# Second FFN of a macaron layer: the next pair's layer norm right behind the first pair's layers, the second tile's down products between the up layers, two table loads moved

## What is computed

```python
x = x + 0.5 * _L0_ffn_ref(_layernorm(x), ...)
x = x + _L0_attn_ref(_layernorm(x), ...)
x = x + 0.5 * _L0_ffn_ref(_layernorm(x), ...)

# the FFN: D_IN 128, D_HID 512
h = jax.nn.silu(_tlin(x, w1_w, w1_s)) * _tlin(x, w2_w, w2_s)
h = jax.nn.gelu(_tlin(h, h1_w, h1_s), approximate=False)
h = jax.nn.gelu(_tlin(h, h2_w, h2_s), approximate=False)
return _tlin(h, w3_w, w3_s)
```

## Time and profile before

| | before |
|---|---|
| median of three runs | 442.1 us |
| the profiled execution, as a run | 442.02 us |
| its span in the trace | 440.3 us |
| PE matmul busy | 371.1 us, 84% |
| DVE busy | 294.8 us, 67% |
| ACT busy | 277.7 us, 63% |
| POOL busy | 41.9 us, 10% |
| chain that ended last | PE 58%, DVE 26%, issue 7%, ACT 7%, DMA 1% |

### The profile page before, as it was taken

One profiled execution on the slowest core, in us unless ns is written; L12 is line 12 of the kernel. 1 busy time (PEld: TensorE's weight loads), 2 busy tenths in 40 slices (PEclk: granted clock), 3 DMA queues, 4 the chain that ended last, 5 costly groups with the idle time before them and its releaser, 6 DMA issues.

```text
span 440.3 us, 9783 instructions
## 1 busy us (share of the span) xinstructions
PE 371.1 (84%) x4132; PEld 278.6 (63%) x4132; DVE 294.8 (67%) x461; ACT 277.7 (63%) x434; POOL 41.9 (10%) x103
## 2 busy tenths in 40 slices
PE   5599999999999998899488489366599687978996
PEld 3377776678866876799377376233267465556885
DVE  2796679628216845699696968667868696578433
ACT  4788956879677776383243265451576838558973
POOL 4000000000000100000788400000000000000000
PEclk9899999999999996889956889585999898989999
DMA  8900007400000000071600001600000000001001
GB/s 272 333 1 2 2 0 227 111 1 1 1 1 0 0 2 3 4 214 49 173 5 4 1 4 36 230 1 1 0 1 3 1 0 2 0 1 49 3 1 48
DMA packets 14325, 19.75 MB, mean 45 GB/s; under 512 B 960, under 2 KB 9152, under 8 KB 14272
## 3 DMA queue, kind: packets, MB, share of 16 engines
q1 hardware_dynamic: 14128, 18.94, 14.4%
q10 hardware_dynamic: 144, 0.01, 0.0%
HBM read 17.91 MB, written 1.05 MB: 43 GB/s over the span
## 4 chain that ended last, share of the span: by engine, by line
PE 58%; DVE 26%; issue 7%; ACT 7%; DMA 1%; DVEq 0%; SPq 0%; ACTq 0%
PE ps_a L723 11%; PE ps_a L724 11%; PE ps_a L827 8%; PE ps_a L894 2%; PE ps_a L884 2%; DVE arena L1074 2%; DVE arena L1071 2%; PE ps_d L794 2%; PE ps_d L858 2%; PE ps_a L917 2%; DVE acts L1121 2%; PE ps_d L724 2%; PE ps_d L723 2%; PE ps_d L894 2%; DVE hbuf L1116 2%
## 5 line engine op out<-in xcount | busy, mean ns | idle before, releaser
L723 PE MATMUL ps_a<-acts,w_f 128*128 128x512 f32 x256 | 103.6, 405 | 9.1 <-ACT acts L597 8.5
L724 PE MATMUL ps_a<-acts,w_f 128*128 128x512 f32 x256 | 101.7, 397 | 0.0
L723 PEld LDWEIGHTS ps_a<-acts,w_f 128*128 128x128 f32 x256 | 49.2, 192 | 22.6 <-ACT acts L597 10.2
L724 PEld LDWEIGHTS ps_a<-acts,w_f 128*128 128x128 f32 x256 | 49.2, 192 | 10.9 <-issue 0.7
L597 ACT ACTIVATE acts<-ps_a,vec 128x512 fp32r<-128x512 f32 x64 | 44.6, 697 | 0.0
L827 PE MATMUL ps_a<-xnp,conv_w 128*128 128x512 f32 x156 | 38.5, 404 | 0.0
L1140 DVE TENSOR_TENSOR acts<-gbuf,acts 128x512 fp32r<-128x512 f32 x32 | 21.6, 689 | 24.9 <-ACT acts L597 24.9
L1140 DVE TENSOR_TENSOR acts<-ghbuf,acts 128x512 fp32r<-128x512 f32 x32 | 21.2, 689 | 20.8 <-ACT acts L597 20.8
L827 PEld LDWEIGHTS ps_a<-xnp,conv_w 128*128 128x128 f32 x156 | 29.3, 188 | 8.2 <-issue 1.4
L987 DVE SCALAR_TENSOR_TENSOR arena<-ps_d,arena 128x512 f32<-128x512 f32 x16 | 11.0, 686 | 30.4 <-ACT arena L551 26.3
L594 ACT ACTIVATE gbuf<-ps_a,vec 128x512 f32<-128x512 f32 x32 | 22.3, 697 | 10.3 <-PE ps_a L724 10.2
(11 more groups left out here) (211 smaller groups left out, 778.5 us busy)
## 6 DMA issues: line engine op xcount, KB each, us to landing
toep<-in_fir SPq DMA_DIRECT2D x24, 288.0 KB, 6.5
w_in<-in_h SPq DMA_DIRECT2D x4, 1024.0 KB, 8.2
g_rows<-in_gW SPq DMA_DIRECT2D x4, 640.0 KB, 6.7
w_in<-in_w SPq DMA_DIRECT2D x6, 256.0 KB, 4.7
iobuf<-in_x SPq DMA_DIRECT2D x4, 256.0 KB, 6.5
toep<-in_taps SPq DMA_DIRECT2D x1, 768.0 KB, 6.7
y<-iobuf SPq DMA_DIRECT2D x3, 256.0 KB, 2.4
toep<-in_proj SPq DMA_DIRECT2D x1, 256.0 KB, 8.6
```

Source lines behind the costliest of these rows:

```text
L723: e.matmul(bank, w, hi, start=start, stop=False)
L724: return e.matmul(bank, w, lo, start=False, stop=stop)
```

## The change

The list of steps of the second FFN is rewritten at the turn from the first pair to the second, and two preloads are put into ACT's walk. Afterwards the steps are: mean 2, var 2, mean 3, var 3, down 0, up 2, down 1, out 0, out 1, up 3, and then as before. ACT loads the table of the reciprocal root ahead of `mean` of tile 2 and the table of silu behind `var` of tile 3. A side effect in unchanged code: where `mean` and `var` of a tile stand next to each other, DVE's L988 frees both their banks at once.

```diff
         else:
-            s += [("up", f, a)] + ([("out", f, 0), ("out", f, 1)] if last else []) + [("up", f, b)]
+            s += [("up", f, a)] + ([("down", f, 1), ("out", f, 0), ("out", f, 1)] if last else []) + [("up", f, b)]
         if more and last:
 
-            s += [("hid1", f, a), ("hid1", f, b), ("hid2", f, a), ("wo", 2, 2), ("wo", 2, 3), ("hid2", f, b), ("down", f, a),
-                  ("mean", f, 2), ("mean", f, 3), ("var", f, 2), ("var", f, 3), ("down", f, b)]
+            s += [("hid1", f, a), ("hid1", f, b), ("hid2", f, a), ("wo", 2, 2), ("wo", 2, 3), ("hid2", f, b),
+                  ("mean", f, 2), ("var", f, 2), ("mean", f, 3), ("var", f, 3), ("down", f, a)]
@@
                 elif kind == "mean":
                     n = NORM_AT[s]
+                    if s == ("mean", 1, 2):
+                        preload(ACT.Abs_reciprocal_sqrt)
@@
+                    if s == ("var", 1, 3):
+                        preload(ACT.Silu)
```

## The result

The changed kernel took 445.69 us (median of 8 runs, 443.52 to 448.15) against 442.05 us for the kernel before (8 runs, 439.83 to 443.51). The ratio is 1.0088, 95% interval 1.0057 to 1.0118: 3.9 us slower, between 2.5 and 5.2. Against the bound of 1% this is "no change that counts", on the slow side.

What follows compares the result with a forecast made beforehand. PE, unbroken from `hid1` of tile 2, was taken to bound the end. Span 440.3 us, plus 1.1 (wait, net of the 2.16 gained) and 1.5 (clock), gave 442.9; plus 1.7, 444.6 us; range 441.8 to 446.4.

Steps and rivals of the forecast that it cites:

- both terms: Start of `hid1` of tile 2 with the 1.1 us wait and the 1.5 us of half clock both counted.
- The wait: `up` 3 on PE queues behind tile 1's transposes, which need DVE's late `down` 1: `hid1` 1.1 us later, net of gain.
- The clock: Half clock on PE behind the new idle stretch, in `up` 3 and `hid1`: 1.5 us more, bounds 0 and 1.6.
- over 3 us: Sign in the changed trace: PE idle this long ahead of the second four transposes; 3.4 us was forecast.
- harmless: Said of `up` 2's last bank of `ps_d` waiting until DVE is through `down` 0; no cost was counted.
- The loads: DVE starts `up` 2 2.16 us earlier: 1.08 from tile 2's root, 1.08 from silu's load; a preload takes 1.40 us.
- The cover of 0.1 us: Tile 3's longer norm chain is ready at 388.86, just hidden behind DVE's work on tile 2 until 388.96.
- The wait alone: Rival: the clock does not fall in the new stretch, or falls before PE goes on; 443.1 us, chance 0.17.
- Twice: Rival: clock also falls behind PE's idle 2.6 us between mean 2 and var 2; 445.6 us, chance 0.23.
- Faster: Rival: the norm chain sets the end, PE does half of `up` 3 early as now; 439.9 us, chance 0.07.
- nothing: Rival: added and gained time cancel, with no half clock or branch gap; about 442 us, chance 0.08.

Runs made afterwards that it cites:

- fill_12: The changed kernel plus 12 matmuls of no use on PE ahead of the second transposes: 443.08 us against 442.78 for the kernel before, ratio 1.0016.
- changed_again: The changed kernel, unaltered, measured a second time against the kernel before: 444.04 us against 441.63, ratio 1.0073.
- norms_paired: The changed kernel with the old order mean 2, mean 3, var 2, var 3: 444.93 us against 441.63 for the kernel before, ratio 1.0066.
- down1_back: The changed kernel with `down` 1 put back ahead of `up` 2, behind `down` 0: 441.32 us against 442.78 for the kernel before, ratio 0.9977.
- down1_only: The kernel before with only `down` 1 moved behind `up` 2, norms and loads as before: 444.18 us against 442.78, ratio 1.0049.

## Why the prediction was right

The forecast was 444.6 us, "same" at 0.88, through a gain of 2.16 us that the new wait and the clock spend. Its steps, each as the time behind the last gelu's start (380.62 in the trace it was made from, 382.31 in the changed one):

| step | forecast | measured |
|---|---|---|
| square of tile 2 | 2.08 | 2.10 |
| root of tile 2 | 3.85 | 3.90 |
| DVE, norm of tile 2 | 5.22 | 5.28 |
| DVE, norm of tile 3 | 8.34 | 8.40 |
| DVE, first product of `up` 2 | 12.15 | 12.18 |
| DVE, `down` 1 | 17.91 | 17.99 |
| PE, second transposes | 18.71 | 18.79 |
| PE, `up` 3 | 19.23 | 19.41 |
| `hid1` of tile 2, both terms | 24.58 | 24.55 |

- **The wait.** 1.1 us forecast, 1.19 us in `fill_12`, where the clock does not fall. Both are net of the gain of 2.1 us. Right, and caused by `down` 1's place: put back, the kernel is faster than before.
- **The clock.** 1.5 us forecast, 1.39 us by `fill_12` against the changed trace, 1.21 against `changed_again`. It fell behind the idle stretch in all three traces that have it (changed, again, norms paired). The forecast idle time was 3.4 us, the measured 2.96, just under the "over 3 us" that was to show it. `up` 2's last block waits for DVE's `down` 0 (394.72 in the trace), which I had called harmless, so `down` 1 and the first transposes ended 0.5 us later than I had them. The working was off here as well: 392.77 + 2.6 is 395.4 and not 395.9, and the trace has 3.6 us from DVE's first product (394.49) to PE's last transpose (398.13), since the last block's four matmuls belong to it. This did no harm to the time, because DVE and not PE sets when the second transposes start. And 2.96 us is still as long as the 2.92 and 2.86 us behind which the clock had fallen before the change, so the term stood.
- **The loads.** 2.16 us forecast; the preloads alone give 2.08 in the stretch, and 2.7 (1.8 to 3.5) in time. `down1_back`, 1.5 expected, gave 1.49 in the stretch and 1.0 (0.0 to 1.9) in time. The price of a load was 1.40 us as the row had it (383.01 to 384.41), not the 2.66 us of the Trainium skill, "ScalarE: Activation LUTs", What ACT_TABLE_LOAD costs: its extra drain shows in no trace here.
- **The cover of 0.1 us.** ACT's second step for tile 3 started at 389.98, DVE's norm at 390.71, 0.73 later where it needs 0.66. It held by 0.07 us, and in `norms_paired` the order makes no difference that can be measured.
- **Size.** In time the change cost 3.9 and 3.2 us, in the traced stretch 2.6 and 2.4. Both intervals (from 2.5 and from 2.0 us) reach down to it. Whether the rest is chance or a second fall of the clock in some executions is open, as told above. The 1.7 us by which the changed trace was late ahead of the last gelu are in code that is the same, and are not counted to the change.
- **The rivals.** "The wait alone" is what `fill_12` makes of the kernel: 0.7 us (-0.6 to 2.0) over the kernel before in time. "Twice" is in no trace: behind the idle 2.50 us the clock stayed at 1.00. "Faster" and "nothing" did not come: DVE took `down` 1 where its order has it.

## What to carry to other kernels

The place of a step in a shared list is its place on every engine. Matmuls that fill a gap on PE may put their consumer on DVE behind a long step, and what waits for that consumer stands ahead of everything else on PE. Before a step is moved, follow the result that it makes to its last reader and ask what is queued behind that reader. Of a change with several parts, time each alone: here the preloads alone gave 2.7 us, and with the reordering the kernel was 3.2 to 3.9 us slower than before.

## What was not expected of the hardware

Twelve matmuls of no use made a kernel faster in the traced stretch by 1.4 us, because PE's clock stayed at 1.00 where it had been 0.51. Behind the idle 2.50 us ahead of tile 2's `var` the clock stayed at 1.00 in all four traces that have it (changed, again, `down1_back`, `fill_12`). Ahead of the second transposes PE stood 2.96, 2.95 and 2.78 us in three traces (changed, again, `norms_paired`), and each time the clock fell behind it. In `down1_only`, where PE stood 5.39 us, it fell while PE was still idle and stayed at 0.50 for 6.8 us.
